# Second attention: one projection for all heads, stacks built by DMAs, 52-row score products

## The reference, cut to what matters

```python
q = split_heads(x @ Wq + bq)
k = split_heads(x @ Wk + bk)
v = split_heads(x @ Wv + bv)
attn = jnp.einsum('bhqd,bhkd->bhqk', q, k) / jnp.sqrt(jnp.float32(HEAD_DIM))
alibi = -slopes[:, None, None] * (Tx - 1 - jnp.arange(Tx, dtype=jnp.float32))[None, None, :]
attn = attn + alibi
attn = jnp.where(causal, attn, jnp.finfo(jnp.float32).min)
p = jax.nn.softmax(attn, axis=-1)
out = jnp.einsum('bhqk,bhkd->bhqd', p, v).transpose(0, 2, 1, 3).reshape(Bx, Tx, C)
return out @ Wo + bo
```

## Time and profile before

| | |
|---|---|
| time, median of 3 runs | 1968.56 us (1966.62 to 1972.32) |
| span of the profiled execution | 1965.4 us |
| TensorE busy | 1807.3 us |
| VectorE, ScalarE, POOL busy | 1183.1, 1017.7, 733.9 us |
| mean granted clock of TensorE | 0.970 |

### The profile page before, as it was taken

How to read it: one execution, slowest core, us unless ns; L and a number is a source line. 1 busy time by engine, 2 the same in 40 slices (tenths; PEclk the granted TensorE clock), 3 DMA queues, 4 the chain that set the end, 5 groups by cost and what they waited for, 6 DMA issues and landing times.

```text
span 1965.4 us, 35109 instructions
## 1 busy us (share of the span) xinstructions
PE 1807.3 (92%) x11362; PEld 1457.0 (74%) x11362; DVE 1183.1 (60%) x2506; ACT 1017.7 (52%) x2134; POOL 733.9 (37%) x652
## 2 busy tenths in 40 slices
PE   5999999998989999869989999999898999997898
PEld 4888888887856565558868888888877666555787
DVE  6667676764277777612366676767533777775124
ACT  4665565653346665424346655565533566654333
POOL 2644454444511111035436444445554111111353
PEclk9999999999989999989999999999998999998899
DMA  3000000001110010151011000000012000101410
GB/s 127 15 22 15 22 13 21 15 2 44 46 55 12 32 37 1 31 118 48 25 45 36 11 26 1 13 22 15 17 41 65 33 22 11 37 1 48 117 48 30
DMA packets 47595, 65.84 MB, mean 33 GB/s; under 512 B 5872, under 2 KB 36464, under 8 KB 45168
## 3 DMA queue, kind: packets, MB, share of 16 engines
q1 hardware_dynamic: 47472, 64.29, 10.7%
HBM read 61.07 MB, written 3.21 MB: 33 GB/s over the span
## 4 chain that ended last, share of the span: by engine, by line
PE 63%; issue 17%; DVE 9%; ACT 5%; POOL 4%; DMA 0%; DVEq 0%; SPq 0%; ACTq 0%; POOLq 0%
PE ps L332 16%; PE ps L334 15%; PE ps L333 15%; PE ps L774 4%; PE ps L788 3%; PE ps L751 3%; PE ps L633 2%; DVE nmax L1309 2%; ACT E L989 2%; POOL E L1596 1%; ACT PT_h L971 1%; PE ps L761 1%; PE ps L572 1%; DVE On L1251 1%; PE ps L800 1%
## 5 line engine op out<-in xcount | busy, mean ns | idle before, releaser
L989 ACT ACTIVATE E<-ps,nmax 128x128 f32<-128x128 f32 (+7 forms) x256 | 189.1, 742 | 207.8 <-DVE nmax L1309 207.1
L1369 DVE TENSOR_TENSOR Hf<-ps,silu_g 128x512 f32<-128x512 f32 x96 | 66.4, 691 | 306.7 <-PE ps L334 180.9
L1593 POOL TENSOR_SCALAR E<-E,mixc 128x128 f32<-128x128 f32 (+7 forms) x128 | 97.7, 763 | 383.4 <-DVE mixc L1279 383.4
L1101 ACT ACTIVATE PT<-ps 128x512 f32<-128x512 f32 (+3 forms) x384 | 178.5, 488 | 104.5 <-PE ps L776 58.6
L1309 DVE TENSOR_REDUCE nmax<-ps 128x1 f32<-128x128 f32 (+7 forms) x256 | 183.4, 749 | 14.0 <-PE ps L610 13.8
L1579 POOL TENSOR_TENSOR H_l<-Hf,H_h 128x512 fp32r<-128x512 f32 x96 | 124.4, 1297 | 176.7 <-ACT H_h L1054 176.4
L332 PE MATMUL ps<-XT_h,Fw_h 128*128 128x512 f32 x384 | 157.5, 410 | 33.1 <-POOL Fw_l L1579 21.2
L1596 POOL TENSOR_TENSOR E<-E 128x128 f32<-128x128 f32 (+7 forms) x128 | 182.7, 1427 | 10.7
L1408 DVE TENSOR_REDUCE nmax_part<-ps 128x1 f32<-128x512 f32 (+3 forms) x256 | 140.3, 585 | 58.0 <-PE ps L751 57.3
L332 PE MATMUL ps<-V_h,PT_h 128*128 128x256 f32 x576 | 169.7, 295 | 0.0
L333 PE MATMUL ps<-V_l,PT_h 128*128 128x256 f32 x576 | 163.9, 285 | 0.0
(11 more groups left out here) (213 smaller groups left out, 5200.9 us busy)
## 6 DMA issues: line engine op xcount, KB each, us to landing
Fw_raw<-in_fa SPq DMA_DIRECT2D x48, 256.0 KB, 2.6
Wa_raw<-in_wa SPq DMA_DIRECT2D x9, 1024.0 KB, 5.0
alibi<-in_alibi SPq DMA_DIRECT2D x8, 1024.0 KB, 4.7
comb_bc<-combs SPq DMA_DIRECT2D x16, 512.0 KB, 12.2
Wo_raw<-in_wo SPq DMA_DIRECT2D x8, 512.0 KB, 3.7
Wb_raw<-in_wb SPq DMA_DIRECT2D x8, 512.0 KB, 4.3
Fw_raw<-in_fb SPq DMA_DIRECT2D x32, 128.0 KB, 2.5
Xn<-in_x SPq DMA_DIRECT2D x3, 1024.0 KB, 5.7
```

Of the source, the lines that this page charges most:

```text
L989: nc.scalar.activation(e[:, 0:w], ps[m][:, 0:w], ACT.Exp, bias=nmax[:, s % 4, m:m + 1], accum_out=lsum[:, s % 4, m:m + 1]).then_inc(exp_do ...
L1101: nc.scalar.activation(PT[:, n, a - (z - HALF):], ps[1][:, n % 2 * HALF + a - (z - HALF):(n % 2 + 1) * HALF], ACT.Exp, scale=SCALE1).then_ ...
L1593: nc.gpsimd.tensor_scalar(e2, e2, mixc[:, n % 4:n % 4 + 1], 1.0, ALU.mult, ALU.mult).then_inc(mix_scaled, 1)
```

## The change

Queries and keys of all 16 heads are projected ahead of the first head in eight units (`project1`: q of heads 0 to 7, k of heads 0 to 7, then of heads 8 to 15, each in two halves of the rows), and split at once into QK_h (ScalarE) and QK_l (VectorE). SP then builds the stacks: for each head six DMAs of 16 rows from QK_h and QK_l, and two of 4 rows from DRAM for the maximum and ALiBi rows (`load_stack`). QS and KS have four slots of two heads each; heads 8 to 15 take the place of heads 0 to 7. A score product runs over the 52 rows of its head alone, which start at partition 0 or 64. The output is a product of OTs with a 128 x 32 matrix that selects and adds (rsel), so VectorE has no sums to make. Vs holds all heads and is written by the bias addition. The heads are written out one by one, without a loop.

```diff
-    Vs = sb("Vs", [P, NT, 4, 32], F32, s)
-    QS = sb("QS", [P, 4, T], F32R, s)
+    Vs = sb("Vs", [P, NT, HEADS1, 32], F32, s)
...
+        QK_h = sb("QK_h", [P, 4, T], F32R, s)
+        QK_l = sb("QK_l", [P, 4, T], F32R, s)
+        QS = sb("QS", [P, PAIRS1, T], F32R, s)
+        KS = sb("KS", [P, PAIRS1, T], F32R, s)
...
-        order = """t0 t1 a0 uk0 uq0 a1 o0 t2 a2 a3 n1 t3 o1 a4 zk0 zq0 uk1 a5 t4 t5 uq1 v0 t6 a6 a7 t7 n0 zq1 t8 zk1 a8
-                   a9 t9 v1 t10 a10 t11 a11 v2 c0 c1""".split()
+        order = """t0 t1 a0 a1 o0 t2 a2 a3 n1 t3 a4 a5 t4 t5 v0 t6 a6 a7 t7 n0 t8 a8 a9 t9 v1 t10 a10 t11 a11
+                   v2 c0 c1""".split()
...
-              """V0 uk0 uq0 zk0 zq0 V1 uk1 uq1 V2 zk1 V3 zq1 V4 V5 a0 a1 a2 a3 V6 a4 a5 a6 a7 V7 a8 a9 n0
-                 a10 a11""".split()]
+              """U0 U1 V0 V1 U2 U3 V2 V3 U4 U5 V4 V5 U6 U7 V6 V7 a0 a1 a2 a3 a4 a5 a6 a7 a8 a9 n0 a10 a11""".split()]
+
+    def unit1(n):
+
+        return 2 * (n // 4) + n % 2, n // 2 % 2
+
+    def slot_rows(h, n=ROWS1):
+
+        return slice(h % 2 * SLOT1, h % 2 * SLOT1 + n)
...
+        def load_stack(b, p):
+
+
+            half, slot = p // PAIRS1, p % PAIRS1
+            if slot == 0:
+                sp.wait_ge(u_lo, 8 * b + 4 * half + 4)
+            for h in (2 * p, 2 * p + 1):
+                at, heads = h % 2 * SLOT1, slice(h % 8 * D1, h % 8 * D1 + D1)
+                if half:
+                    sp.wait_ge(t_ready, PIECES1 * (HEADS1 * b + h - 2 * PAIRS1 + 1))
+                done = stack_in[h % (2 * PAIRS1)]
+                q, k = 2 * half, 2 * half + 1
+                for dst, row, src in ((QS, at, QK_h[heads, q]), (KS, at, QK_h[heads, k]), (QS, at + D1, QK_l[heads, q]),
+                                      (KS, at + D1, QK_h[heads, k]), (QS, at + ROWS1 - D1, QK_h[heads, q]),
+                                      (KS, at + ROWS1 - D1, QK_l[heads, k])):
+                    sp.dma_start(dst[row:row + D1, slot].bitcast(F32), src.bitcast(F32)).then_inc(done, 16)
+                for dst, src in ((QS, d["qrows"]), (KS, d["krows"][h])):
+                    sp.dma_start(dst[at + MAX_ROW:at + MAX_ROW + 4, slot].bitcast(F32), src).then_inc(done, 16)
...
+        sp.dma_start(ramp[:], d["ramp"]).then_inc(ramp_in, 16)
         load_x(0)
-        for t, src in ((ident, "ident"), (mask_raw, "mask"), (bsel, "bsel"), (subln, "subln")):
+        for t, src in ((ident, "ident"), (mask_raw, "mask"), (bb, "bb"), (rsel, "rsel"), (subln, "subln")):
...
+        sp.wait_ge(rows_ready, 3)
+        for r in range(2):
+            sp.dma_start(d["krows"][:, r], ones[:]).then_inc(rows_out, 16)
+        sp.dma_start(d["krows"][:, 2:4], ramp_hl[:].bitcast(F32)).then_inc(rows_out, 16)
+        sp.dma_start(d["qrows"][0:2], zeros[:]).then_inc(rows_out, 16)
+        sp.dma_start(d["qrows"][2:4], ones[0:2]).then_inc(rows_out, 16)
         sp.wait_ge(w2_out, 16)
+        sp.wait_ge(rows_out, 80)
...
+        def project1(b, n):
+
+            if n == 0:
+                pe.wait_ge(wb_lo, b + 1)
+            if n >= 2:
+                pe.wait_ge(u_lo, 8 * b + n - 1)
+            r, h = unit1(n)
+            w, x = tile(r // 2 + r % 2 * 2), tile(h, HALF)
             for c in range(KC):
-                mm = pass3(pe, bank, Wb_h[:, c, w], Wb_l[:, c, w], XT_h[:, c, n], XT_l[:, c, n], c == 0, c == KC - 1)
+                mm = pass3(pe, ring[n % 2], Wb_h[:, c, w], Wb_l[:, c, w], XT_h[:, c, x], XT_l[:, c, x], c == 0, c == KC - 1)
             mm.then_inc(u_mm, 1)
...
+            if k == 0:
+                pe.wait_ge(stack_in[h % (2 * PAIRS1)], 16 * STACK_LOADS * (2 * b + h // (2 * PAIRS1) + 1))
...
-            bank = ps[0][:, tile(k % 2, HALF)]
-            mm = nc.tensor.matmul(bank[:, 0:scored - a], QS[:, j, tile(i)], KS[:, j // 2, a:scored], start=True, stop=True)
+            bank, slot, at = ps[0][:, tile(k % 2, HALF)], h // 2 % PAIRS1, slot_rows(h)
+            mm = nc.tensor.matmul(bank[:, 0:scored - a], QS[at, slot, tile(i)], KS[at, slot, a:scored], start=True, stop=True)
...
-                mm = nc.tensor.matmul(bank[:, n - base:], KS[:, j // 2, tile(kb)], QS[:, j, n:z], start=True, stop=True)
+                n, slot, at = min(a, z - 2 * P), h // 2 % PAIRS1, slot_rows(h)
+                mm = nc.tensor.matmul(bank[:, n - base:], KS[at, slot, tile(kb)], QS[at, slot, n:z], start=True, stop=True)
...
-                for t in range(4):
-                    mm = nc.tensor.transpose(ps[3][:, HALF + t * P:HALF + (t + 1) * P], OTs[:, tile(4 * h + t)], ident[:])
+                pe.wait_ge(o1_done, H + 1)
+                for half in range(2):
+                    pe.wait_ge(ots_done[half], H + 2)
+                for t in range(NT):
+                    mm = nc.tensor.matmul(ps[3][:, HALF + tile(t, 32).start:HALF + tile(t, 32).stop], OTs[:, tile(t)], rsel[:],
+                                          start=True, stop=True)
                 mm.then_inc(o_ps, 1)
...
-                nc.vector.tensor_reduce(osum[:, tile(h, 4), 0:D1 + 1],
-                                        ps[3][:, HALF:].rearrange("p (t c e) -> p t e c", t=4, c=4)[:, :, 0:D1 + 1, :],
-                                        AX.X, ALU.add).then_inc(o_used, 1)
...
+        dve.wait_ge(ramp_in, 16)
+        nc.vector.memset(ones[:], 1.0)
+        nc.vector.memset(zeros[:], 0.0).then_inc(rows_ready, 1)
+        nc.vector.tensor_copy(ramp_hl[:, 0], ramp[:]).then_inc(rows_ready, 1)
+        dve.wait_ge(rows_ready, 2)
+        nc.vector.tensor_tensor(ramp_hl[:, 1], ramp[:], ramp_hl[:, 0].bitcast(F32), ALU.subtract).then_inc(rows_ready, 1)
...
-            fills = [(QS[:, j].bitcast(F32), 0.0) for j in range(4)] + [(nmax1_cols[:].bitcast(F32), 0.0), (Vs[:], 1.0)]
+            fills = [(nmax1_cols[:].bitcast(F32), 0.0), (Vs[:], 1.0)]
...
-            split_wb(b * GROUPS1)
-            for h in range(2):
-                stack1(0, h, b * GROUPS1)
-            pool.wait_ge(qs_zero, 6 * b + 6)
-            pool.wait_ge(v1_done, NT * b + NT)
-            for j in range(4):
-                head_values(j, j * D1)
-            with pool.Fori(0, GROUPS1 - 1) as g:
-                attn1_group(b, g)
-            for h in range(2):
-                stack1(1, h, b * GROUPS1 + (GROUPS1 - 1))
+            split_wb(b)
             pool.wait_ge(xt_ps, LN_B // 2 * b + 12)
             add_bias(X, 1)
```

More of the change, by code:

```diff
@@ L91, in program @@
     eps_col = sb("eps_col", [P, 1])
-    bsel = sb("bsel", [P, 2])
+    bb = sb("bb", [P, 4])
+    rsel = sb("rsel", [P, 32])
     rbias = sb("rbias", [P, EXPERTS])
@@ L297, in program @@
     v1_done = sem("v1_done")
-    vs_done = sem("vs_done")
     wb_hi = sem("wb_hi")
     wb_lo = sem("wb_lo")
-    bb_in = sem("bb_in")
+    ramp_in = sem("ramp_in")
+    rows_ready = sem("rows_ready")
+    rows_out = sem("rows_out")
     u_mm = sem("u_mm")
[L303 to L308, removed]
+    u_hi = sem("u_hi")
+    u_lo = sem("u_lo")
+    stack_in = [sem(f"stack_in{i}") for i in range(2 * PAIRS1)]
     o_zero = sem("o_zero")
@@ L491, in _ @@
             sp.dma_start(Rw_raw[:], d["rw"]).then_inc(rw_in, 16)
[L492 to L501, removed]
+            sp.dma_start(Wb_raw[:], d["wb"]).then_inc(wb_in, 16)
+            for p in range(2 * PAIRS1):
+                load_stack(b, p)
             for c in range(2):
@@ new lines, in project1, with max_rows @@
+        def project1(b, n):
+            r, h = unit1(n)
+            act.wait_ge(u_mm, 8 * b + n + 1)
+            nc.scalar.activation(QK_h[:, r, tile(h, HALF)], ring[n % 2], ACT.Identity, bias=bb[:, r:r + 1]).then_inc(u_hi, 1)
+        def max_rows(b, h, half):
+            rows = slice(h % 2 * SLOT1 + MAX_ROW, h % 2 * SLOT1 + MAX_ROW + 2)
+            act.wait_ge(nt_ps, 2 * (HEADS1 * b + h) + half + 1)
+            nc.scalar.copy(QS[rows, h // 2 % PAIRS1, tile(half, HALF)], ps[3][rows, 0:HALF]).then_inc(n_done, 1)
@@ new lines, in attn1_head @@
+        def attn1_head(b, h):
+            H = HEADS1 * b + h
+            for kind, n in slot1(h):
+                if kind == "t":
+                    kb, a, z = t_piece(n)
+                    if n % 4 == 0:
+                        act.wait_ge(pv1_done, 3 * H + n // 4 + 1)
+                    act.wait_ge(t_ready, PIECES1 * H + n + 1)
+                    nc.scalar.activation(PT[:, n, a - (z - HALF):], ps[1][:, n % 2 * HALF + a - (z - HALF):(n % 2 + 1) * HALF],
+                                         ACT.Exp, scale=SCALE1).then_inc(t_used, 1)
+                elif kind == "n":
+                    max_rows(b, h + 1 - n, n)
+                elif kind == "c" and n == 0:
+                    act.wait_ge(pv1_done, 3 * H + 1 + 3)
+                    nc.scalar.copy(OTs[:, 0:HALF], ps[2][:, 0:HALF]).then_inc(ots_done[0], 1)
@@ L1385, in ffn_out, with project1 @@
             add_norm(b, k, bank, lambda t: ring[t // 2][:, tile(t % 2, HID)])
[L1387 to L1401 removed]
+        def project1(b, n):
+            r, h = unit1(n)
+            dve.wait_ge(u_hi, 8 * b + n + 1)
```

(30 more changed lines are left out.)

301 lines of the change are left out of this document (73 added, 228 removed).

## The result

The changed kernel takes 2385.25 us (median of 4 runs, 2383.4 to 2386.68), the kernel before 1968.72 us beside it: a ratio of 1.2117, 95% interval 1.2101 to 1.2133. The forecast was 2024 us, range 1893 to 2080. The direction was right, the size was not: +416.5 us in place of +55.1.

The account below looks back on a forecast made before the run. TensorE was taken to bound the kernel. Terms -97.5 + 28.2 + 118.1 + 3.6 + 2.7 = +55.1 us, on a span of 1965.4 plus 3.2, gave 2024 us, 2.8% slower; range 1893 to 2080.

Parts of the forecast that it names:

- Score pieces over 52 rows: TensorE's score products in the heads: 984 changes of tile shape at 0.12 us each, +118.1 us.
- the overlap of pieces: Two adjacent pairs per head of different heads' pieces, in different array halves, may overlap: left as a bound of -12 us.
- the period of the forecast: Time between VectorE's copies of OTs: 16.3 us if right (11.58 + 0.88 + 3.84), about 12.5 if changes are free.
- The price of a change: Each change of tile shape on TensorE costs 0.12 us, bounds 0 and 0.20; break-even at 0.064 us.
- The first rival: A change of rows costs nothing, so the sum lacks 118.1 us: 1906 us, faster; chance 0.34.
- The projections: Projections leave the heads, so heads fall to the plain period of 11.58 us, last 9.54: -97.5 us.
- The outputs: Eight plain f32 products per head replace transposes, eight more loads, 0.88 us per head: +28.2 us; bounds 0 and +2.1 per head.
- Ahead of the heads: Projection units and transposes before the first score piece: +1.8 us per batch, +3.6 us in all, bounds 0 and +5.
- The DMAs: Head 0's stack lands at 565.3, just ahead; later heads need 3.9 us of SP per 11.6 us or more.
- The start: Two more loads ahead of the constants and VectorE's memsets, copy and subtraction: +2.7 us, bounds 1 and 5.
- its 1906: Time in us forecast for the case without a cost for changes of shape, -63.0 us.
- The signs named for "wrong": Pieces and masks 0.04 us apart, a wait for stack_in ahead of a head, or a period set by VectorE or ScalarE.

Follow-up runs that it names:

- kernel with few stops: Changed kernel with each mask product only over the 64 rows of the head's own slot, leaving out half the causal mask: 2068.85 us, measured once.
- the outputs of before: all-128-row kernel with eight transposes a head and VectorE's two sum reductions in place of the selection products: 1902.68 us, ratio to before 0.9664.
- all-128-row kernel: Changed kernel with score products over all 128 rows again, the other slot's rows zero, all else as changed: 1950.54 us, ratio to before 0.9914.
- run with plain waits: all-128-row kernel with each score piece waiting until VectorE has read the piece right before it, not the one before that: 2224.11 us, measured once.

## Why the prediction was wrong, point by point

**The step that failed is "Score pieces over 52 rows".** It priced the change of shape, 984 x 0.12, from rows that were all read at the high clock, and took the clock of before over into the kernel after without asking what holds it. No rival had it either; the range of 1893 to 2080 was made of prices of stops and outputs at the high clock. The runs show that the same stops, and the rows left idle, bring the granted clock from 1.00 to 0.50 for 437 us in each batch. Undoing the 52 rows gives back 434.7 us. Of these, 984 x 0.094 = 92 to 984 x 0.108 = 106 us are the changes' price at the high clock, and the overlap of pieces takes at most 31 x 0.84 = 26 us off the 92. So 329 to 369 us are the clock. That is an account, not a measurement: no run kept the changed kernel at 2.4 GHz. By it the kernel would take 1950.5 + 66 = 2017 to 1950.5 + 106 = 2057 us there. A second estimate agrees with the upper end: the head of 27.13 us, divided by the 1.66 between the levels in the kernel with few stops, is 16.3 us, the period of the forecast. That the 2024 us lie in this span is in part luck, since a price that was rather high made up for the terms below that were too low.

**The price of a change** was right in kind and a little high: 0.094 and 0.108 us in two kernels, 0.12 forecast, and it comes with a change of rows as with one of columns. The first rival, that rows change free of cost, is refuted: it would have left 0.04 us behind a mask, and 0.16 is seen. The overlap shows in the changed kernel in the two pairs of a head that the forecast named; how many of the 12 us allowed for it came is not shown. The 0.84 us a head are of a kernel whose masks overlap too.

**The projections** (-97.5): the periods on which the term rests were right to the hundredth. With the outputs of before the heads take 11.58 us and the last 9.54; only the second and third differ, at 11.93 and 11.22 us, and they make up for each other.

**The outputs** (+28.2) cost 47.9, inside the bound of 2.1 us a head. The loads' distance was right; that a plain head loses 1.29 us and not 0.88, and that the last loses 2.97, was missed.

**Ahead of the heads** (+1.8 a batch) was too low: the first piece starts at 580.92 us against 565.34, of which 6.9 are the start, so 8.7 us in the first batch. Two rows of TensorE's timeline of the changed kernel, answering to the earlier trace rows:

```profile
553.94 0.79 PE L331 MATMUL ps<-XT_h,Wb_h 128*128 128x512 f32 x1 [2.19 <-DVE XT_l L1160]
...
565.97 0.79 PE L331 MATMUL ps<-XT_h,Wb_h 128*128 128x512 f32 x1 [5.33 <-DVE XT_l L1160]
```

The first is U0, the second U2. U0 to V1, in part at 1.2 GHz (mean granted clock 0.75 from 553.9 to 560 us), run past the moment when the second half of X is ready, its transposes come late, and U2 waits 5.33 us for the split. ScalarE copies this half ahead of its work on U0, so it waits for the transposes, and VectorE, which needs ScalarE's part first, sits idle for 6.69 us with its work on U0, U1, V0 and V1 still ahead of the split:

```profile
562.00 1.41 DVE L1370 SCALAR_TENSOR_TENSOR QK_l<-ps,bb,QK_h 128x512 fp32r<-128x512 f32 x2 [6.69 <-ACT QK_h L1067]
```

The step named the transposes' new place and missed what ScalarE and VectorE have queued around them. The DMAs were as forecast: no wait for a stack in the changed kernel. The all-128-row kernel waits 3.1 us a batch, since its first product needs two heads' stacks.

**The start** (+2.7, bounds 1 and 5) was 6.9 us by the second attention. VectorE's four operations on the constant rows and the first K_l:

```profile
34.60 0.91 DVE L1500 MEMSET ones<- 16x1024 f32 x1 [0.27 <-DVE neglam L1496]
35.67 0.91 DVE L1501 MEMSET zeros<- 2x1024 f32 x1 [0.16 <-issue]
36.51 0.62 DVE L1502 CAST ramp_hl<-ramp 16x1024 fp32r<-16x1024 f32 x1
37.16 1.21 DVE L1504 TENSOR_TENSOR ramp_hl<-ramp,ramp_hl 16x1024 fp32r<-16x1024 f32 x1
38.31 2.71 DVE L1210 SCALAR_TENSOR_TENSOR K_l<-ps,ba,K_h 128x512 fp32r<-128x512 f32 x4
```

The operations last what was forecast, and K_l is 5.13 us later than in the earlier trace rows, and x's first low part is 3.1 us later (17.81 against 14.73 us), where the forecast had 1.0 for the loads ahead of it.

These terms also account for the 44 us by which the all-128-row kernel missed its 1906: 47.9 - 28.2 for the outputs, 2 x (8.7 - 1.8) ahead of the heads (the second batch taken like the first), 6.9 - 2.7 at the start and 2 x 3.1 for its own wait, 43.9 us in all.

**The signs named for "wrong"** were a wait for a stack, pieces 0.04 us behind masks, or a period set by another engine. None came. The one that did, the clock, was not on the list.

## What to carry to other kernels

Read the granted clock beside every price, and ask of a change what it does to how fully TensorE's array is used: idle rows, pauses at changes of shape and waits all counted here, and a price read at 1.00 holds only while the clock stays there. Zeros in unused rows are not waste where they keep a product at 128 rows and its shape that of its neighbours: here that is worth 434.7 us. When a good idea comes in a bundle, undo its parts one at a time: the early projection, the DMA-built stacks and the heads without a loop are together worth 67 us, with what they cost at the start taken off (1969.5 for before in that comparison, 1902.68 with them), and the 52 rows and the new outputs hid that.

## What the runs showed of the hardware that was not expected

- With TensorE busy throughout by the profile, its granted clock was 0.81 and 0.78 (160 of 160 us) and 0.50 (60 of 60), where it was 1.00 for the same work over 128 rows without the changes of shape. The Trainium skill's list of rules in "TensorE: Matmul & The Clock Gate", section "Why this matters for your kernels", names idle gaps between bursts of matmuls as what makes throughput drop in a kernel; in the run with plain waits the clock falls though no wait in the head stage is over 0.8 us, and the others show the fall with hardly a gap in the profile. The measurements go beyond that rule.
- Rows of zeros did not lower the clock: the kernel before multiplies 64 of them in each score product at 1.00, and without them, with the changes of shape that this brings, its clock was 0.83. Fewer rows with few changes gave 0.65.
- The price of a change of shape was 0.094 and 0.108 us at 2.4 GHz, for a change of rows.
- 52-row products in different halves of the array run at the same time, both within 0.49 us for 512 columns, in a kernel whose masks keep to these halves too. Its head was 0.84 us shorter at the high clock; its mean clock was 0.65.
